# A two-layer graph kernel: earlier gathers, a product moved behind the last sums, and the feature halves formed inside the sweep

## The chip, the cores and the metric

One core of a Trainium2 chip runs the whole program. The metric is the device time of one execution in microseconds (us), as the median of three.

## The reference, cut to what matters

3125 nodes with 128 features, 103125 edges sorted by their target `dst`. Two layers follow each other:

```python
# layer 0
deg  = segment_sum(ones, src);  d = where(deg > 0, rsqrt(deg), 0)
h    = x @ weight
out0 = segment_sum((d[src] * d[dst])[:, None] * h[src], dst) + bias
x    = layernorm(x + out0)
# layer 1
w_ij  = mlp(edge_attr_64) + mlp(edge_attr_32)        # silu(x @ w0 + b0) @ w1 + b1
alpha = ((x @ wq)[dst] * w_ij * (x @ wk)[src]).sum(heads) / sqrt(16) * edge_weight
out1  = segment_sum(alpha * (x @ wv)[src], dst) / 16
x     = layernorm(x + out1)
```

## The kernel before, in words

The program has five stages. Engines run their own instruction streams and meet at semaphores; PE is the matrix engine, DVE the vector engine, ACT the scalar engine, POOL the GpSimd, SP a queue that only issues DMAs.

**Head (0 to 88 us).** The source degrees are counted with one-hot products (DVE line 1323, PE line 1033). DVE and ACT form `xs`, the features of all 25 blocks of 128 nodes times `dinv` (lines 1349 and 858), and ACT's queue stores them to `xs_d` in four DMAs (lines 862 and 865, semaphore `s_xs`). POOL prepares rows and the split of the MLP weights (lines 732 to 772). DVE decides how many passes a sweep needs (`passes_i`, one for these inputs, line 1376); every engine loads that number into a register before its loop. ACT rounds all of `xs` into `xs_hi` (line 873, 128x3200, fp32r) and loads the Silu table (line 874). DVE forms the rest `xs_lo = xs - xs_hi` in 13 instructions (line 1405), and then `start_pass1` (lines 1413 to 1428) writes rows, keys and bases of the pass; its last semaphore step `s_pass1` lets POOL start.

**Sweep 1 (88 to 568 us).** The sum of layer 0 over the edges, and a quarter of the MLP work of layer 1 on top, in 51 steps written out one behind the other. Of the 808 tiles of 128 edges, 358 are *gathered*: POOL issues one indirect DMA for each (line 794, seven a step, eight in the last), which fetches 128 rows of `xs_d` into one of four buffers `gath1`, and PE adds them with a one-hot product (`sum1`, line 1092), whose window DVE adds to `acc` (line 1468). The other 450 tiles are *counted*: DVE writes two one-hots for each (`hots`, lines 1475 and 1476), PE multiplies them into counts (`count_batch`, line 1114), DVE adds these into `count` (line 1492). In every eighth step and in the last, PE multiplies the counts with `xs_hi` and `xs_lo` (`sum_spans`, line 1122, 50 matmuls, "the product"), DVE adds the three windows (`add_spans`), and ACT sets the three parts of `count` back to zero in this and the next two steps (`clear_counts`, line 930). The MLP of a step: SP loads the edge features, ACT and DVE split them (`split_hi` line 892, `split_lo` line 1454), PE `layer1` (lines 1066, 1068), ACT Silu (line 900), PE `layer2` (line 1084), ACT copies out (line 919), puts the bias into the bank again (line 884), SP stores to `w_d` (line 529).

POOL's order is: wait for the pass rows, then for each step wait for the indices (`s_idx1`) and, from the fifth step on, for the sum four steps back (`s_sum1`), then issue. SP loads the indices of a step (line 536) behind the features of the step before it.

In the last step the order on PE is product, `layer2`, `sum1`, `layer2`. The next stage waits on PE for the sums, the spans and the last copy to `w_sb`.

**Middle (568 to 630 us).** DVE makes the rows of sweep 2 (lines 1564 to 1570 and 1433). PE multiplies `acc` with the weight (`convolve`, line 1163), DVE adds and takes statistics (line 1604), ACT normalizes, PE transposes and projects, SP stores `kv_d` and `q_d`.

**Sweep 2 (630 to 1668 us)** and the **end**: attention over 202 groups of 512 edges, then the second normalization. The change does not touch them.

## Time and profile before

| | |
|---|---|
| median of 3 runs | 1691.49 us (1691.41 to 1692.15) |
| the profiled execution's own time | 1685.36 us |
| its span, first to last instruction | 1683.5 us |
| PE busy | 1535.1 us (91%) |
| DVE busy | 1356.2 us (81%) |
| POOL busy | 1215.7 us (72%) |
| ACT busy | 955.0 us (57%) |
| mean granted clock of PE | 0.980 |

Busy shares are averages over stages with different limits, so the stretch in question is read by itself. The profiled execution lies 6.13 us below the median.

### The profile page before, as it was taken

The page shows a single profiled execution, that of the slowest core. Times are in us where ns is not written, and L with a number is a line of the kernel's source. Part 1 is how long each engine was busy: PE and PEld are TensorE (multiplying, and loading weights), DVE is VectorE, ACT ScalarE, POOL GpSimd, SP SyncE. Part 2 cuts the span into 40 slices and gives each one's busy share as a digit, 9 for nine tenths or more (in the row PEclk, how much of TensorE's full clock was granted, in tenths as well). Part 3 has the DMA queues.
Part 4 walks back from the last instruction along what each step waited for, and adds up shares of the span by engine and source line. Part 5 has one row for each costly group of instructions (what it writes and reads, how often), then busy time and mean ns, then how long its engine had stood idle before and what let it go on. Part 6 is the DMA issues. An engine that isn't in the chain of part 4 may idle for free.

```text
span 1683.5 us, 43509 instructions
## 1 busy us (share of the span) xinstructions
PE 1535.1 (91%) x12636; PEld 1426.1 (85%) x12636; DVE 1356.2 (81%) x3810; ACT 955.0 (57%) x1410; POOL 1215.7 (72%) x1201
## 2 busy tenths in 40 slices
PE   4379999999999759999999999999999999999995
PEld 3267988888898749998989898989898989898995
DVE  9988779797887457887888787888787878887886
ACT  3344646566565465665656565655555656565664
POOL 5677777777777247777777777777777777777772
PEclk9999999999999889999999999999999999999998
DMA  4133334343433286666666666666666666666673
GB/s 123 39 97 108 109 102 116 108 121 103 116 108 97 64 231 170 189 190 172 186 183 184 174 186 173 185 182 180 180 180 180 184 178 185 181 186 179 183 190 115
DMA packets 176755, 257.32 MB, mean 153 GB/s; under 512 B 80278, under 2 KB 91213, under 8 KB 176476
## 3 DMA queue, kind: packets, MB, share of 16 engines
q0 software_dynamic: 50240, 129.44, 29.1%
q1 hardware_dynamic: 123100, 124.61, 25.0%
q10 hardware_dynamic: 3264, 1.64, 0.3%
q8 instruction: 48, 0.79, 0.2%
q14 instruction: 103, 0.84, 0.2%
HBM read 232.76 MB, written 22.79 MB: 152 GB/s over the span
## 4 chain that ended last, share of the span: by engine, by line
PE 66%; POOL 13%; issue 8%; DVE 7%; DMA 3%; ACT 1%; DVEq 1%; SPq 1%; POOLq 0%; ACTq 0%
PE bank L1084 33%; POOL arena L794 13%; PE bank L1092 12%; PE bank L1066 9%; PE bank L1068 4%; PE bank L1122 3%; PE bank L1218 3%; DVE arena L1323 2%; DMA arena<-xs_d,idx 1%; DMA idx<-in_src_e 1%; PE bank L1114 1%; DVE xsplit L1454 1%; DVE late L1670 1%; ACT nodes L948 0%; DVE red L1687 0%
## 5 line engine op out<-in xcount | busy, mean ns | idle before, releaser
L784 POOL DMA_INDIRECT arena<-kv_d,idx x808 | 802.5, 993 | 273.2 <-issue 259.8
L1084 PEld LDWEIGHTS bank<-w,hid 128*128 128x128 f32 x6464 | 781.9, 192 | 27.2 <-issue 1.9
L1084 PE MATMUL bank<-w,hid 128*128 128x128 f32 x6464 | 790.9, 276 | 0.0
L900 ACT ACTIVATE hid<-bank,b 128x512 f32<-128x512 f32 x808 | 500.6, 683 | 273.1 <-PE bank L1068 260.2
L794 POOL DMA_INDIRECT arena<-xs_d,idx x358 | 354.6, 991 | 128.8 <-issue 124.5
L1066 PE MATMUL bank<-xsplit,w_hi 128*128 128x512 f32 x808 | 347.7, 441 | 26.3 <-DVE xsplit L1454 26.3
L1454 DVE TENSOR_TENSOR xsplit<-xraw,xsplit 64x256 fp32r<-64x256 f32 x808 | 288.0, 414 | 7.3 <-ACT xsplit L892 1.0
L1092 PE MATMUL bank<-onehot,late 128*128 128x126 f32 x1616 | 219.2, 285 | 33.6 <-DVE late L1708 31.7
L1092 PEld LDWEIGHTS bank<-onehot,late 128*128 128x128 f32 x1616 | 196.7, 195 | 36.9 <-DVE late L1708 33.6
L892 ACT ACTIVATE xsplit<-xraw 64x1024 fp32r<-64x1024 f32 x202 | 210.7, 1044 | 2.6 <-DMA xraw<-in_sph_t 1.7
L884 ACT ACTIVATE bank<-b_full 128x512 f32<-128x512 f32 x199 | 119.3, 599 | 160.4 <-DVE late L1708 158.8
L1066 PEld LDWEIGHTS bank<-xsplit,w_hi 128*128 128x128 f32 x808 | 157.5, 195 | 50.1 <-DVE xsplit L1454 24.5
L1661 DVE TENSOR_SCALAR late<-late,iota_part 126x512 bf16<-126x512 bf16 x202 | 71.0, 352 | 115.5 <-PE bank L1218 113.9
L1068 PE MATMUL bank<-xsplit,w_lo 128*128 128x512 f32 x404 | 163.8, 405 | 0.0
L1492 DVE TENSOR_TENSOR count<-count,bank 128x300 f32 x225 | 103.9, 462 | 59.9 <-PE bank L1114 46.4
L1670 DVE TENSOR_TENSOR late<-arena,bank 128x512 f32<-128x512 f32 x202 | 137.8, 682 | 7.0 <-PE bank L1218 5.4
L1682 DVE TENSOR_TENSOR late<-late,bank 128x512 f32<-128x512 f32 x151 | 103.0, 682 | 47.8 <-issue 32.7
L1476 DVE TENSOR_SCALAR key_hot<-iota_key,key 128x300 bf16<-128x300 bf16 x450 | 140.9, 315 | 0.0
L1687 DVE TENSOR_REDUCE red<-late 128x32 f32<-128x512 f32 x202 | 137.1, 679 | 0.1
L919 ACT ACTIVATE w_sb<-bank 128x512 f32<-128x512 f32 x51 | 30.5, 598 | 163.3 <-PE bank L1084 163.3
L1475 DVE TENSOR_SCALAR low_hot<-iota_key,low_f 128x128 bf16<-128x128 bf16 x450 | 117.7, 262 | 3.2 <-issue 3.1
L1092 PE MATMUL bank<-onehot,arena 128*128 128x126 f32 x716 | 93.2, 278 | 17.3 <-DMA arena<-xs_d,idx 17.1
(159 smaller groups left out, 1358.6 us busy)
## 6 DMA issues: line engine op xcount, KB each, us to landing
xraw<-in_rad_t SPq DMA_DIRECT2D x207, 128.0 KB
xraw<-in_sph_t SPq DMA_DIRECT2D x414, 64.0 KB
late<-relrow_d SPq DMA_DIRECT2D x103, 256.0 KB, 3.9
w_sb<-w_d SPq DMA_DIRECT2D x52, 256.0 KB
w_d<-w_sb SPq DMA_DIRECT2D x51, 256.0 KB
arena<-kv_d,idx POOLq DMA_INDIRECT x808
arena<-xs_d,idx POOLq DMA_INDIRECT x358
qwin<-q_d SPq DMA_DIRECT2D x101, 31.5 KB
```

Of the source, the lines that this page charges most:

```text
L784: pool.indirect_dma_start(gath[:, k, t * width:(t + 1) * width], None, table, bass.IndirectOffsetOnAxis(ap=idx[:, pair.slot(4), j * TILES ...
L794: pool.indirect_dma_start(gath1[s.slot(RING1)][:, t * D:(t + 1) * D], None, xs_d, bass.IndirectOffsetOnAxis(ap=idx[:, s.slot(4), t:t + 1], ...
L892: act.activation(xsplit[0:RAD, s.slot(2), :, :], xraw[:, k, :, :], ACT.Copy).then_inc(mlp.s_hi, 1)
L900: act.activation(hid[:, s.slot(2), c, :], hid_ps[s.sub(4, c, 4 * s.total).slot(len(hid_ps))][:, :], ACT.Silu, bias=b0[:, c:c + 1]).then_in ...
L1066: mm = pe.matmul(to, w0_hi[:, m, cols], xsplit[:, b, m, :], start=True, stop=(m == 1))
L1068: mm = pe.matmul(to, w0_lo[:, m, cols], xsplit[:, b, m, :], start=False, stop=True)
L1084: mm = pe.matmul(w_ps[:, t * D:(t + 1) * D], hid[:, b, c, t * P:(t + 1) * P], w1[:, c, :], start=False, stop=(c == 3), skip_group_check=True)
L1092: return pe.matmul(bank[7][:, 0:3 * WIN], rows, onehot[:, b, k:k + 3, :].rearrange("p t n -> p (t n)"), start=(k == 0), stop=(k == n - 1), ...
L1454: last = dve.tensor_tensor(xsplit[RAD:P, b, m, half], xraw[:, k, m, half], xsplit[0:RAD, b, m, half].bitcast(F32), ALU.subtract)
L1476: last = dve.tensor_scalar(key_hot[:, at_tile + t, :], iota_key[:, :], key[:, ds(col, 1)], None, ALU.is_equal)
L1670: dve.tensor_tensor(prod[:, j, :].rearrange("p (t f) -> p t f", t=TILES), kv(g)[:, :, 0, :], q_ps[j][:, :].rearrange("p (t f) -> p t f", t ...
L1687: dve.tensor_reduce(red[:, j, :, :].rearrange("p t h -> p (t h)"), prod[:, j, :].rearrange("p (h d) -> p h d", d=HD), AX.X, ALU.add).then_ ...
```

## The change

- POOL no longer waits for the pass rows before its first gather. The wait stands before the fourth step's gathers, whose buffer shares memory with what `start_pass1` writes. The wait for `s_xs`, the stored features, stays.
- `xs_hi` is rounded in two parts, blocks 0 to 14 by POOL (behind its weight split, before its register load) and blocks 15 to 24 by ACT (before the two casts of the halves). The half indices now live in `w_sb`, since `xs_hi` shares memory with where they were.
- `xs_lo` is formed by DVE inside the sweep, in 13 instructions over the steps 1, 2 and 3. PE waits for it before a product, no longer before the sweep.
- DVE splits the features of steps 0 and 1 before `start_pass1`. ACT loads the Silu table behind its first two splits. PE does all of `layer2` of step 0 before the counts and the sum.
- In the last step PE does `layer2`, `sum1`, `layer2` first and the product last. DVE adds the last window, makes the rows of sweep 2 (`rows_of_sweep2`) and then adds the spans. ACT clears the third part of `count` for the product of step 48 in step 49, not in step 50.

```diff
@@ late / w_sb
-        half_i, to = part_i(late, to, 2 * DENSE)
+        half_i, _ = part_i(w_sb[:, :, :].rearrange("p k f -> p (k f)"), 0, 2 * DENSE)
@@ POOL
+            pool.wait_ge(s_cast, CAST.rows)
+            pool.wait_ge(s_pre, PRE.xs + 1)
+            own = slice(0, XS_ACT[0])
+            pool.tensor_copy(xs_hi[:, own, :], xs_sb[:, own, :]).then_inc(s_round, 1)
             pool.wait_ge(s_pre, PRE.passes)
             n_pass1 = passes(pool, 1)
             pool.wait_ge(s_xs, 64)
...
                 if not s.before(RING1):
                     pool.wait_ge(s_sum1, (s - RING1).tick + 1)
+                if s.c == RING1 - 1:
+                    pool.wait_ge(s_pass1, s.p * PASS1 + PASS1)
                 pool.sem_inc(s_go, 1)
...
             with pool.Fori(0, n_pass1) as p:
-                pool.wait_ge(s_pass1, p * PASS1 + PASS1)
                 steps1(sweep1, p)
@@ ACT
+            act.wait_ge(s_xsa, NB - XS_ACT[0])
+            act.wait_ge(s_cast, CAST.rows)
+            own = slice(XS_ACT[0], NB)
+            act.activation(xs_hi[:, own, :], xs_sb[:, own, :], ACT.Copy).then_inc(s_round, 1)
             act.wait_ge(s_pre, PRE.half)
             act.activation(low_f[:, :], half_i[:, 0, :], ACT.Copy).then_inc(s_cast, 1)
             act.activation(hi8[:, :], half_i[:, 1, :], ACT.Copy, scale=float(NARROW)).then_inc(s_cast, 1)
-            act.wait_ge(s_pre, PRE.xs + 1)
-            act.wait_ge(s_xsa, NB - XS_ACT[0])
-            act.wait_ge(s_cast, CAST.all)
-            act.activation(xs_hi[:, :, :], xs_sb, ACT.Copy).then_inc(s_table, 1)
-            act.activation(table[:, :], b0[:, 0:1], ACT.Silu).then_inc(s_table, 1)
...
                     split_hi(s + 1, mlp)
+                    if mlp is mlp1:
+                        act.activation(table[:, :], b0[:, 0:1], ACT.Silu).then_inc(s_table, 1)
                     silu(s, mlp)
...
-                for j in reversed(range(SPANS)):
-                    k = product(s - j) if s.c >= j else None
-                    if k and (j < OPEN or not k.is_last()):
+                for c in range(s.c - SPANS, s.c + 1):
+                    k = product(Step(c, p=s.p, total=UNITS)) if c > 0 else None
+                    for j in range(OPEN if k and k.is_last() else SPANS if k else 0):
+                        if min(c + j, max(c, UNITS - 2)) != s.c:
+                            continue
@@ PE
-            pe.wait_ge(s_split, 1)
...
-            def sum_spans(added):
+            def sum_spans(added, p):
                 pe.wait_ge(s_add, added)
+                pe.wait_ge(s_split, p + 1)
...
                 if s.before(1):
                     layer1(s, mlp1)
+                    layer1(s + 1, mlp1)
+                    layer2(s, mlp1, w1_ps[0])
+                    count_batch(own[0])
+                    count_batch(own[1])
+                    sum1(s)
+                    for batch in own[2:]:
+                        count_batch(batch)
+                    return
                 if s.is_last():
+                    layer2(s, mlp1, w1_ps[0], range(2))
+                    sum1(s)
+                    layer2(s, mlp1, w1_ps[0], range(2, 4))
+                    pe.wait_ge(s_acc1, s.tick + 1)
+                    pe.wait_ge(s_zero, s.p * CLEARS + CLEARS - OPEN)
+                    sum_spans((s.p + 1) * COUNTED, s.p)
+                    return
...
@@ DVE
-            dve.wait_ge(s_xs, 64)
-            dve.wait_ge(s_table, 1)
-            for b in range(0, NB, 2):
-                own = slice(b, min(NB, b + 2))
-                last = dve.tensor_tensor(xs_lo[:, own, :], xs_sb[:, own, :], xs_hi[:, own, :].bitcast(F32), ALU.subtract)
-            last.then_inc(s_split, 1)
...
+            def low_xs(s):
...
+                for b in range(2 * (s.c - 1), NB, 6):
+                    own = slice(b, min(NB, b + 2))
+                    last = dve.scalar_tensor_tensor(out=xs_lo[:, own, :], in0=xs_hi[:, own, :].bitcast(F32), scalar=minus[:, 0:1],
+                                                    in1=xs_sb[:, own, :], op0=ALU.mult, op1=ALU.add)
...
+                if s.is_last():
...
+                    add_window(bases[0], WIN, sum1_ps, s_sum1, s.tick + 1, s_acc1, s.tick)
+                    rows_of_sweep2(s.p)
+                    dve.wait_ge(s_acc1, s.tick + 1)
+                    add_spans(product(s), span_bases)
+                    return
...
+                if 1 <= s.c <= 3:
+                    low_xs(s)
...
             with dve.Fori(0, n_pass1) as p:
+                head = Step(0, p=p, total=UNITS)
+                split_lo(head, mlp1)
+                split_lo(head + 1, mlp1)
                 start_pass1(p)
```

The instruction order shows three places. First ACT ahead of the sweep, before:

```order
L868 ACTIVATE low_f<-late 128x450
L869 ACTIVATE hi<-late 128x450
L873 ACTIVATE xs_hi<-arena 128x3200
L874 ACT_TABLE_LOAD
L874 ACTIVATE table<-b 128x1
L434 TENSOR_LOAD passes_i
L434 ISA x2
L879 ACTIVATE b_full<-bank 128x128
```

And with the change:

```order
L879 ACTIVATE xs_hi<-arena 128x1280
L881 ACTIVATE low_f<-w_sb 128x450
L882 ACTIVATE hi<-w_sb 128x450
L438 TENSOR_LOAD passes_i
L438 ISA x2
L887 ACTIVATE b_full<-bank 128x128
L944 UNCONDITIONAL_BRANCH
L944 ISA
L900 ACT_TABLE_LOAD
L900 ACTIVATE xsplit<-xraw 64x1024
```

The rounding is smaller and comes first; a table load now stands before the first `xsplit`, and the one for Silu follows the second `xsplit`.

Second, ACT from the last Silu of step 49 to the end of the sweep, before:

```order
L900 ACTIVATE hid<-bank,b 128x512
L930 ACTIVATE count<-count 128x2800
L918 REGISTER_ALU
L919 ACTIVATE w_sb<-bank 128x512
L884 ACTIVATE bank<-b_full 128x512
L930 ACTIVATE count<-count 128x2800
```

And with the change:

```order
L908 ACTIVATE hid<-bank,b 128x512
L942 ACTIVATE count<-count 128x2800 x2
L928 REGISTER_ALU
L929 ACTIVATE w_sb<-bank 128x512
L892 ACTIVATE bank<-b_full 128x512
```

Two clears now stand before the copy and the bias of step 49. In step 50 one clear is left, before the last copy to `w_sb`, as before.

Third, PE in the last step with the change (before, the 50 matmuls of the product stood ahead of the first of these rows):

```order
L1095 MATMUL bank<-w,hid 128x128 x4
L1103 MATMUL bank<-onehot,arena 128x126 x8
L1093 REGISTER_ALU
L1095 MATMUL bank<-w,hid 128x128 x4
L1093 REGISTER_ALU
L1095 MATMUL bank<-w,hid 128x128 x4
L1155 ISA
```

The product follows the last row.

## Rows read from the trace of the kernel before

**Rows 1.** POOL in order of time: start us, us, engine line op.

```profile
87.80 1.31 POOL L794 DMA_INDIRECT arena<-xs_d,idx  x1 [20.01 <-issue]
...
550.20 0.97 POOL L794 DMA_INDIRECT arena<-xs_d,idx  x1 [0.30 <-issue]
```

**Rows 2.** The gathers' line, 85 to 570 us: ns min/median/max, first and last start.

```profile
L794 POOL DMA_INDIRECT arena<-xs_d,idx x358: 951/955/1427, 87.8 to 550.2; - x179
```

**Rows 3.** PE in order of time, `sum1` of steps 9, 11 and 47.

```profile
177.61 1.73 PE L1092 MATMUL bank<-onehot,arena 128*128 128x126 f32 x14
...
193.16 1.73 PE L1092 MATMUL bank<-onehot,arena 128*128 128x126 f32 x14
...
524.72 0.93 PE L1092 MATMUL bank<-onehot,arena 128*128 128x126 f32 x6 [1.41 <-DMA arena<-xs_d,idx]
```

**Rows 4.** Waits, 85 to 560 us: PE's for the gathered rows.

```profile
PE bank L1092 <- DMA arena<-xs_d,idx: 17.1, 16, 1.8
```

**Rows 5.** DVE in order of time, head and start of the sweep.

```profile
68.13 2.23 DVE L1349 TENSOR_TENSOR arena<-nodes,dinv 128x896 f32<-128x896 f32 x2
...
74.21 0.13 DVE L1378 TENSOR_SCALAR passes_i<-small 1x1 int32<-1x1 f32 x1
...
78.05 4.31 DVE L1405 TENSOR_TENSOR rounded<-arena,xs_hi 128x256 fp32r<-128x256 f32 x13 [1.32 <-ACT xs_hi L873]
82.28 0.23 DVE L1413 TENSOR_SCALAR base_i<-base_f,off 1x51 int32<-1x51 f32 x1
...
86.12 0.63 DVE L1428 TENSOR_TENSOR key<-key,arena 128x450 f32<-128x450 f32 x1
```

**Rows 6.** The stores of `xs_d` from ACT's queue: issue and landing.

```profile
L865 ACTq DMA_DIRECT2D xs_d<-arena x2: 566/879/1192, 69.7 to 71.4; - x2
...
DMA to landing us min/median/max: 3.8/4.6/5.4
```

**Rows 7.** POOL's elementwise instructions up to 80 us, busy us and mean ns.

```profile
L768 POOL TENSOR_TENSOR w_lo<-w_raw,w_hi 128x512 fp32r<-128x512 f32 x1 | 32.5, 32477 | 12.0 <-ACT w_hi L849 12.0
...
L746 POOL TENSOR_SCALAR key<-tile_f 128x450 f32<-128x450 f32 x1 | 1.6, 1607 | 0.1
...
L705 POOL CAST iota_key<-arena 128x300 bf16<-128x300 f32 x1 | 0.4, 435 | 0.1
```

**Rows 8.** PE in order of time, end of sweep 1.

```profile
550.94 0.68 PE L1114 MATMUL bank<-key_hot,low_hot 128*128 128x300 bf16 x4
...
562.85 1.95 PE L1084 MATMUL bank<-w,hid 128*128 128x128 f32 x16
...
566.42 1.95 PE L1084 MATMUL bank<-w,hid 128*128 128x128 f32 x16
569.46 2.04 PE L1163 MATMUL bank<-w_l_sb,acc 128*128 128x128 f32 x16 [1.09 <-ACT w_sb L919]
573.70 1.87 PE L1163 MATMUL bank<-w_l_sb,acc 128*128 128x128 f32 x8 [2.19 <-DVE nodes L1604]
```

**Rows 9.** ACT in order of time, end of sweep 1.

```profile
547.10 2.55 ACT L930 ACTIVATE count<-count 128x2800 fp32r<-128x2800 f32 x1
551.23 0.60 ACT L919 ACTIVATE w_sb<-bank 128x512 f32<-128x512 f32 x1 [1.58 <-PE bank L1084]
563.05 2.54 ACT L930 ACTIVATE count<-count 128x2800 fp32r<-128x2800 f32 x1 [8.14 <-PE bank L1122]
568.49 0.60 ACT L919 ACTIVATE w_sb<-bank 128x512 f32<-128x512 f32 x1 [2.90 <-PE bank L1084]
```

**Rows 10.** DVE in order of time, end of sweep 1.

```profile
567.50 0.28 DVE L1565 TENSOR_SCALAR base_f<-base_f,small 128x101 f32<-128x101 f32 x1
...
572.08 0.60 DVE L1604 SCALAR_TENSOR_TENSOR nodes<-bank,dinv,nodes 128x128 f32<-128x128 f32 x2
```

**Rows 11.** PE and its granted clock (third number) just before the sweep's end.

```profile
552.00:560.00 8.00, 4.96 (x32) 1.00 0.10 38
```

**Rows 12.** The chain of waits, the sweep's end: PE's last product.

```profile
555.04 7.97 PE bank L1122 x50
```

More of the change, by code:

```diff
@@ L241, in build @@
         small = sb("small", [P, 16])
+        minus = sb("minus", [P, 1])
         dinv = sb("dinv", [P, NB])
@@ L344, in build @@
         s_split = sem("s_split")
+        s_round = sem("s_round")
+        s_minus = sem("s_minus")
+        s_early = sem("s_early")
         s_biased = sem("s_biased")
@@ L1099, in sum1 @@
                     pe.wait_ge(s_acc1, s.tick)
-                if product(s):
+                if product(s) and not s.is_last():
                     pe.wait_ge(s_wide, (product(s).tick + 1) * SPANS)
@@ L1129, in sweep1 @@
                     layer1(s, mlp1)
-                if s.is_last():
-                    pe.wait_ge(s_acc1, s.tick)
-                    pe.wait_ge(s_zero, s.p * CLEARS + CLEARS - OPEN)
-                    sum_spans((s.p + 1) * COUNTED)
-                else:
-                    layer1(s + 1, mlp1)
-                    count_batch(own[0])
-                    if product(s):
-                        pe.wait_ge(s_acc1, s.tick)
-                        sum_spans(own[0].tick)
-                    count_batch(own[1])
+                    layer1(s + 1, mlp1)
[6 more added lines that the diff above has]
+                    return
+                if s.is_last():
+                    layer2(s, mlp1, w1_ps[0], range(2))
[5 more added lines that the diff above has]
+                    return
+                layer1(s + 1, mlp1)
+                count_batch(own[0])
+                if product(s):
+                    pe.wait_ge(s_acc1, s.tick)
+                    sum_spans(own[0].tick, s.p)
+                count_batch(own[1])
                 layer2(s, mlp1, w1_ps[0], range(2))
@@ L1397, in _ @@
             pre(dve.tensor_tensor(near[:, :], dst_f[:, COLS1:COLS], tile_f[:, :], ALU.subtract))
+            dve.memset(minus[:, :], -1.0).then_inc(s_minus, 1)
             v = pre(dve.memset(off[:, :], 0.0))
[L1401 to L1406 removed]
             pre_wait(v)
@@ L1493, in add_counts @@
                                   ALU.add).then_inc(s_add, 1)
+            def low_xs(s):
+                if s.c == 1:
+                    dve.wait_ge(s_xs, 64)
+                    dve.wait_ge(s_round, 2)
+                    dve.wait_ge(s_minus, s.p + 1)
+                for b in range(2 * (s.c - 1), NB, 6):
+                    own = slice(b, min(NB, b + 2))
+                    last = dve.scalar_tensor_tensor(out=xs_lo[:, own, :], in0=xs_hi[:, own, :].bitcast(F32), scalar=minus[:, 0:1],
+                                                    in1=xs_sb[:, own, :], op0=ALU.mult, op1=ALU.add)
+                if s.c == 3:
+                    last.then_inc(s_split, 1)
+                    dve.wait_ge(s_split, s.p + 1)
+                    dve.memset(minus[:, :], 0.0).then_inc(s_minus, 1)
@@ new lines, in rows_of_sweep2 @@
+            def rows_of_sweep2(p):
+                dve.tensor_scalar(base_f[:, :], base_f[:, :], small[:, 3:4], None, ALU.mult).then_inc(s_early, 1)
+                dve.tensor_scalar(small[0:PAIRS, 4:5], relrow0[:, 0, 0:1], small[0:PAIRS, 3:4], None, ALU.mult).then_inc(s_early, 1)
+                dve.wait_ge(s_early, p * EARLY + 2)
+                dve.tensor_tensor(by_pair(rel0[:, :]), by_pair(dst_f[:, :]), pair_bcast(base_f[:, :]), ALU.subtract).then_inc(s_early, 1)
+                dve.tensor_scalar(relrow0[:, :, :], relrow0[:, :, :], small[0:PAIRS, 4:5], None, ALU.subtract).then_inc(s_early, 1)
+                dve.wait_ge(s_early, p * EARLY + 4)
+                dve.tensor_scalar(relrow[:, :, :], relrow0[:, :, :], float(PARTS), None, ALU.mult).then_inc(s_early, 1)
+                dve.wait_ge(s_early, p * EARLY + 5)
@@ L1495, in sweep1 @@
             def sweep1(s):
                 own = batches(s)
+                if s.is_last():
+                    bases = load(base1_i, s.n, 1, NP - 1)
+                    span_bases = load(span_i, (product(s) * SPANS).n, SPANS, NP - 1)
+                    dve.wait_ge(s_acc1, s.tick)
+                    add_window(bases[0], WIN, sum1_ps, s_sum1, s.tick + 1, s_acc1, s.tick)
[3 more added lines that the diff above has]
+                    return
@@ L1497, in sweep1 @@
                 if s.before(1):
                     one_hot(s, GATHERED, tiles1(s)).then_inc(s_hot1, 1)
-                    split_lo(s, mlp1)
-                    split_lo(s + 1, mlp1)
                     for j in range(HOTS):
@@ L1562, in _ @@
                 dve.wait_ge(s_zero, p * CLEARS + CLEARS)
-            v_off = pre(dve.memset(off[:, :], 0.0))
-            v = pre(dve.tensor_scalar(base_f[:, :], base_f[:, :], small[:, 3:4], None, ALU.mult))
-            v_rb = pre(dve.tensor_scalar(small[0:PAIRS, 4:5], relrow0[:, 0, 0:1], small[0:PAIRS, 3:4], None, ALU.mult))
-            pre_wait(v)
-            pre(dve.tensor_tensor(by_pair(rel0[:, :]), by_pair(dst_f[:, :]), pair_bcast(base_f[:, :]), ALU.subtract))
-            pre_wait(v_rb)
-            v = pre(dve.tensor_scalar(relrow0[:, :, :], relrow0[:, :, :], small[0:PAIRS, 4:5], None, ALU.subtract))
-            pre_wait(v)
-            next_rows()
+            dve.memset(off[:, :], 0.0).then_inc(s_rows, 1)
+            dve.wait_ge(s_rows, 1)
             def statistics(c, row, s_row, rows_done, s_bn, s_mv):
@@ L1815 @@
 PASS2 = 3
+EARLY = 5
 class PRE:
```

## The prediction

> **What bounds the kernel now.** Busy shares come first on the page, and they mislead: PE is busy 91% of the span, but the part that the change touches is sweep 1 with its head and tail. There I read POOL in order of time. It issues its first gather at 87.80 us after 20.01 us of idleness, and its last at 550.20 [rows 1]. These are 358 gathers [rows 2], so 357 intervals of (550.20 - 87.80) / 357 = 1.295 us, while a single gather takes 0.955 us at the median and 0.30 us lie between two [rows 1, 2]. So POOL issues without a break for 463 us: a step of seven gathers is 9.07 us, and eight steps are 72.5.
>
> PE then: `sum1` of step 9 begins at 177.61 and of step 11 at 193.16 [rows 3], that is 7.78 us a step where it waits for nothing, and a product takes 7.9 [rows 12]. Eight steps with one product cost PE 8 x 7.78 + 7.9 = 70.1 us, 2.4 less than POOL. It falls behind at each product and catches up: all in all it waits 17.1 us for gathered rows [rows 4], and the last such wait is in step 47 (1.41 us, [rows 3]). From there the tail runs on PE alone. So the bound of sweep 1 is when POOL starts, plus 358 gathers, plus the tail behind step 47. PE, DVE and ACT only have to keep up.
>
> **The start.** The first gather comes 87.80 - 86.75 = 1.05 us after the last instruction of `start_pass1` [rows 1, 5]. With the change that wait is gone and the next condition is `s_xs`. Its last store is issued at 71.4 and lands at most 5.4 us later [rows 6], at 76.8. `passes_i` is written at 74.34 [rows 5], so POOL has 2.5 us for its register load. With the same 1.05 us the first gather starts at 77.9: **9.9 us earlier**. The new wait before the fourth step asks for `start_pass1`, done near 86, and POOL gets there at 77.9 + 3 x 9.07 = 105, so it costs nothing.
>
> POOL first has to round 1920 columns. It can begin at 70.4, when DVE has written its part of `xs` (68.13 + 2.23, [rows 5]). The nearest row is a cast with one input, 300 columns in 0.435 us [rows 7], which makes 2.8 us in proportion and ends at 73.2, before 74.34: nothing. The far end is the scalar operation on 450 columns in 1.61 us [rows 7]: 6.9 us, ending at 77.3, which with a register load of 1 to 2 us costs 2 us, or up to 4.6 if DVE's small instructions meanwhile wait for it. I take zero, since the cast is the same kind of operation. The Trainium skill (GPSIMD Engine Reference, section 3.1, elementwise) has one-input bodies at 1.03 cycles an element, an estimate of 1.7 us; the result would be the same.
>
> **Gathers beside more DVE work.** The first gather takes 1.31 us beside `split_lo`, against 0.951 at the least [rows 1, 2], 0.36 extra. Now they run beside `start_pass1` too (4.5 us, from 82.28 to 86.75 [rows 5]), and in steps 1 to 3 beside 13 more instructions of 0.33 us (4.31 / 13, [rows 5]). At 0.2 us for about five gathers, I take **1.0 us** lost; bounds 0 and 3. The rule against the change is in the Trainium skill (SBUF — State Buffer, "SBUF: two separate sides"): while DVE runs in a two-port mode, GpSimd cannot write the descriptors of its DMAs at all. By that rule the first gathers would lose all the one-input time of `start_pass1`, an estimate of 2.6 us, and the sum would be 1.6 worse. The first gather's 0.36 us beside a run of DVE work says that it is less here.
>
> **PE and DVE at the start.** ACT gets a table load ahead of its first split, so the splits are ready near 79 and 80. DVE splits until 81.8, then `start_pass1` until 86.3, and starts its one-hots only 3 us earlier than before, while POOL is 9.9 ahead. PE's `layer1` starts near 80.4, `layer2` of step 0 fills until 90, and `sum1` of step 0 follows when its rows have landed (89). `xs_lo` adds 1.7 us of DVE work to step 1 and 1.3 to each of the two others. DVE is then at some 8.8 us a step against POOL's 9.07, so it neither gains nor loses; from step 4 on PE has 1.3 us of slack a step. POOL itself is held only if PE falls over 10 us behind. Cost: nothing, the cover is PE's 17.1 us of waiting [rows 4]; if that cover were gone, see the second rival. The 13 instructions leave the head, but the head's chain no longer ran over them for POOL: their 4.31 us are inside the 9.9, not added to them.
>
> **The tail.** In times of before: PE's counts end at 551.6 (550.94 + 0.68, [rows 8]). Both clears now stand ahead of the copy of step 49 on ACT: 547.10 + 2 x 2.55 = 552.2, then copy 0.60 and bias 0.60 [rows 9], so `layer2` of step 50 starts at 553.45. `layer2`, `sum1`, `layer2` take 1.79 each (562.85 to 566.42 is two of them, [rows 8]), until 558.85; the gathers have landed. The product ends 7.9 later, at 566.75. On ACT the clear of 2.54 us still stands between the product and the last copy, and this is late next: before, the copy waited for `layer2` and ended at 569.09 [rows 9]; now it ends at 566.85 + 2.54 + 0.6 = 570.05. `convolve` follows 0.37 behind it as before (569.46 - 569.09): 570.4, **1 us later** than before. But DVE was not ready before 572.08, since it made the rows of sweep 2 from 567.50 on (4.6 us, [rows 10]); these lie in the shadow of the product now. DVE's first row waits for half of the 2.04 us of `convolve` [rows 8]: 571.45. So 4.6 us of row work and 3.4 us of PE's idleness are taken away, and **0.6 us** comes out. If the granted clock falls during PE's new 3.6 us of idleness, eight of these matmuls cost 1.87 instead of 1.02 [rows 8], and 0.25 us is lost instead. Behind the idleness of 3.4 us before the product the granted clock was 1.00, that is 2.4 GHz [rows 11]; I take no fall.
>
> Sum: -9.9 + 1.0 - 0.6 = **-9.5 us**. The profiled execution's own 1685.36 becomes 1675.9, and the median, 6.13 above it, 1691.49 - 9.5 = 1682.0. Middle and sweep 2 move as a whole.
>
> **The rivals.**
> 1. *POOL's rounding is slow or held by DVE.* For it: line 768, also with an fp32r result, took 32.5 us [rows 7] beside DVE's one-hots. If the copy ends near 77.3 or only starts in DVE's gap behind 76.7, the gathers start 2 to 5 us later than 77.9, and the gain is 4.5 to 7.5: about 1685.5. The same page of the Trainium skill on the SBUF has the pair of ports held for a whole instruction by whoever comes first. Against: at 70.4 DVE has reductions with one input. Chance 0.12.
> 2. *PE or DVE becomes the bound of sweep 1.* If the lag from the start is never made up, only DVE's 3 us and PE's 7 count: gain 3 to 7, about 1686.5. Against: 17.1 us of waits. Chance 0.06.
> 3. *Slower: rounding to fp32r on POOL costs what line 768 shows by itself.* 32.48 us for 512 columns is 63 ns a column; 1920 columns are 122 us, from 70.4 to 192. The gathers would start at about 194 instead of 87.8, and the time would be about 1797. It decides from a copy of over 14 us, where the start falls behind 87.8. Against: line 768 ended about when DVE's one-hots did. Chance 0.03.
> 4. *The change doesn't do what it says*: PE stays 8 us behind at the end whatever POOL does, because the last product is too near. That is so before as well and moves along, so I give it 0.02, with 1690.
>
> **How the numbers follow.** Forecast 0.77, with its own range 1680 to 1684.5 from the bounds 0 and 3 of the contention and -0.6 to +0.25 of the tail. Down to 1679.5 and up to 1687.0 takes in rivals 1 and 2. A measurement of this kernel tells 0.2%, 3.4 us, from no change. Faster by more: 0.77 + 0.12 + 0.03 of rival 2 = 0.92. Within: 0.05. Slower: 0.03.
>
> **What would show it.** First gather near 78; POOL's cast under 4 us; last gather near 541; PE's last wait for gathered rows still near step 47; in the tail a product directly behind the last `layer2`, ACT's copy ending 3.3 us behind it, DVE's first row of the middle 0.6 us closer to the last gather (21.9 us before, 21.3 then). Wrong it is if the first gather comes later than 80, if gathers show idle times over 0.30 us in the sweep, or if PE waits for DVE at the first product.

## The result, and the profile after

| | before | after |
|---|---|---|
| median of 5 runs each | 1691.41 us (1690.00 to 1692.15) | 1678.05 us (1675.46 to 1682.64) |
| ratio | | 0.9926, 95% interval 0.9909 to 0.9943 |
| profiled execution | 1685.36 us | 1677.95 us |
| first gather, last gather | 87.80, 550.20 | 78.06, 541.60 |
| DVE's first row of the middle | 572.08 | 564.34 |
| first expansion of queries (PE, start of sweep 2) | 624.39 | 615.22 |

The change gains 13.4 us by these medians. I had forecast 9.5, and a range that ended at 1679.5: faster as forecast, and 1.5 us outside. Later comparisons ran the changed kernel 12 more times and the kernel before 92 more. Over all executions the means are 1679.7 (17) and 1691.1 (97), with a standard deviation of 3 us from one execution to the next on both sides: **11.4 us, give or take 1.5** (95%).

POOL in order of time in the changed kernel (start us, us, line and tiles, idle before), which answers to [rows 1, 7]:

```profile
70.66 1.78 POOL L783 CAST xs_hi<-arena 128x1920 fp32r<-128x1920 f32 x1 [2.74 <-DVE arena L1372]
78.06 1.20 POOL L804 DMA_INDIRECT arena<-xs_d,idx  x1 [5.61 <-issue]
79.56 1.19 POOL L804 DMA_INDIRECT arena<-xs_d,idx  x1 [0.30 <-issue]
...
541.60 0.96 POOL L804 DMA_INDIRECT arena<-xs_d,idx  x1 [0.30 <-issue]
```

The rounding takes 1.78 us and ends 1.9 us before `passes_i` is there. The first gather comes 9.74 us earlier, as worked out. The last comes 8.60 earlier. Its line, and the waits for gathered rows, answer to [rows 2, 4]:

```profile
L804 POOL DMA_INDIRECT arena<-xs_d,idx x358: 948/955/1439, 78.1 to 541.6; - x179
```

```profile
PE bank L1103 <- DMA arena<-xs_d,idx: 11.5, 11, 1.9
```

In the second line the numbers are us in total, times, and the longest. PE waits 11.5 us instead of 17.1, and still catches up behind each product. The tail on PE, with its granted clock, answers to [rows 8, 11]. First PE's order of time, then windows (us, PE busy, granted clock, DMA share, GB/s):

```profile
545.38 2.05 PE L1095 MATMUL bank<-w,hid 128*128 128x128 f32 x16 [1.71 <-ACT bank L892]
547.26 1.95 PE L1103 MATMUL bank<-onehot,arena 128*128 128x126 f32 x16
549.05 1.95 PE L1095 MATMUL bank<-w,hid 128*128 128x128 f32 x16
```

```profile
551.00:556.00 5.00, 5.00 (x35) 1.00 0.00 0
556.00:561.00 5.00, 2.70 (x18) 1.00 0.00 2
561.00:566.00 5.00, 3.56 (x17) 0.66 0.21 68
```

ACT and DVE beside it answer to [rows 9, 10]:

```profile
558.74 2.54 ACT L942 ACTIVATE count<-count 128x2800 fp32r<-128x2800 f32 x1 [13.49 <-PE bank L1134]
561.18 0.58 ACT L929 ACTIVATE w_sb<-bank 128x512 f32<-128x512 f32 x1
```

```profile
552.69 1.67 DVE L1536 TENSOR_SCALAR relrow<-relrow 101x1024 bf16<-101x1024 f32 x1
558.84 0.27 DVE L1486 TENSOR_TENSOR acc<-acc,bank 128x112 f32 x1 [4.48 <-PE bank L1134]
...
564.34 0.61 DVE L1653 SCALAR_TENSOR_TENSOR nodes<-bank,dinv,nodes 128x128 f32<-128x128 f32 x2 [2.76 <-PE bank L1186]
```

(The CAST is the rounding, L929 the copy to `w_sb`, L1653 DVE's first row of the middle.) The order is the forecast one: last sums, product at once behind them, the rows of sweep 2 (549.5 to 554.4) hidden. The product ends at 558.70, the clear and the copy follow it until 561.76, PE starts the middle at 562.14 after 3.44 us of idleness, and here the clock does fall (0.66 in the last window): the first 16 matmuls take 3.54 us where they took 2.04 [rows 8]. From the last gather to DVE's first row it is 22.74 us, not the 21.3 of the forecast.

So up to sweep 2 the two profiled executions differ by 9.2 us, and at the end by 7.4. The medians differ by 13.4. The experiments had to say which of these numbers the change owns.

### The profile page after: what moved, and what is told of

The parts are those of the page before. It is cut to its first block, busy times and chain, and to the rows that moved or that the text cites. A ratio compares the mean times of both kernels' runs of the same rounds, so it can differ in the third digit from the quotient of the medians.

```text
span 1676.1 us, 43517 instructions
## 1 busy us (share of the span) xinstructions
PE 1538.9 (92%) x12636; PEld 1429.3 (85%) x12636; DVE 1361.1 (81%) x3812; ACT 954.0 (57%) x1411; POOL 1217.6 (73%) x1202
## 4 chain that ended last, share of the span: by engine, by line
PE 69%; POOL 11%; issue 7%; DVE 4%; DMA 3%; ACT 2%; DVEq 1%; SPq 0%; POOLq 0%; ACTq 0%
PE bank L1095 35%; PE bank L1103 13%; POOL arena L804 11%; PE bank L1077 9%; PE bank L1079 4%; PE bank L1134 3%; PE bank L1241 3%; PE bank L1125 1%; DMA arena<-xs_d,idx 1%; DMA idx<-in_src_e 1%; DVE xsplit L1472 1%; DVE late L1719 1%; ACT nodes L960 0%; DVE red L1736 0%; DVE late L1757 0%
## 5 line engine op out<-in xcount | busy, mean ns | idle before, releaser
L1719 DVE TENSOR_TENSOR late<-arena,bank 128x512 f32<-128x512 f32 x202 | 137.7, 682 | 6.1 <-issue 4.5
L929 ACT ACTIVATE w_sb<-bank 128x512 f32<-128x512 f32 x51 | 30.5, 598 | 155.6 <-PE bank L1095 155.6
L1757 DVE TENSOR_TENSOR late<-arena,bank 128x512 f32<-128x512 f32 x151 | 102.5, 679 | 0.1
```

Source lines behind the costliest of these rows:

```text
L1719: dve.tensor_tensor(prod[:, j, :].rearrange("p (t f) -> p t f", t=TILES), kv(g)[:, :, 0, :], q_ps[j][:, :].rearrange("p (t f) -> p t f", t ...
```

## The experiments

Each run's median stands against the kernel before, timed on the same chip beside it:

| run | executions | median, us | ratio, 95% interval |
|---|---|---|---|
| before_again | 12 | 1690.26 | 0.9997 (0.9980 to 1.0015) |
| before_early | 12 | 1682.06 | 0.9953 (0.9937 to 0.9970) |
| after_hold | 12 | 1689.22 | 0.9988 (0.9973 to 1.0004) |
| tail_only | 12 | 1689.38 | 0.9988 (0.9975 to 1.0001) |
| early_tail | 6 | 1679.68 | 0.9936 (0.9917 to 0.9955) |
| after_oldtail | 12 | 1687.15 | 0.9970 (0.9952 to 0.9988) |
| after_again | 6 | 1678.05 | 0.9923 (0.9911 to 0.9935) |
| after_third | 6 | 1681.90 | 0.9946 (0.9926 to 0.9966) |
| before_fill | 12 | 1690.54 | 0.9999 (0.9983 to 1.0014) |
| copy_first | 6 | 1679.95 | 0.9938 (0.9913 to 0.9962) |
| before_long | 5 | 1682.74 | 0.9942 (0.9929 to 0.9955) |
| after_long | 4 | 1670.32 | 0.9868 (0.9852 to 0.9884) |
| copy_long | 5 | 1667.11 | 0.9856 (0.9843 to 0.9868) |
| copy_long2 | 5 | 1666.92 | 0.9866 (0.9839 to 0.9893) |
| early_copy_long | 5 | 1667.33 | 0.9870 (0.9844 to 0.9896) |
| late_idx | 5 | 1670.74 | 0.9880 (0.9855 to 0.9906) |

A difference of two means is given below with its 95% interval. The kernels ran on different chips, where the kernel before had means between 1690.2 and 1692.1 us, so 1 or 2 us between two runs of this table can be the chip's.

**Each kernel again.** No edit.

> The kernel before once more, unchanged, for a second profile and its spread. In the first profile the sweep over the 202 groups of the second half (sweep 2) took 1021 us, 45.4 us of it in ten disturbed steps at its loop turns, and that execution was 6.1 us faster than the median of the timed ones. Theory A (the change itself brings about 9 us, and the remaining 4 of the measured 13.4 lie in sweep 2, whose loop turns cost a varying 3 to 6 us each): median near 1691, and this profile shows the start of sweep 2 (first expansion of queries) at 624.4 within 0.3 us, whatever its total time; the total varies with sweep 2 alone. Theory B (head, sweep 1 or middle differ by as much from execution to execution): the first expansion moves by 1 us or more.

Median 1690.26 of 12 (1684.92 to 1695.08); first expansion at 623.86. Beside it and its three neighbours, 29 executions of the kernel before ran from 1683.11 to 1695.80. The 0.7 us between the three runs that the forecast was made on had been luck.

> The changed kernel once more, unchanged. The kernel before, run 29 times, has spread from 1683.1 to 1695.8 with a median of 1690.9. Theory A (the change brings about 9 us; the 13.4 of the first comparison was luck of five runs on each side, since each execution carries a varying sum from the ten loop turns of sweep 2): this median comes back between 1680.5 and 1683. Theory B (the change brings 13 us): 1678 again. In its profile first gather 78.1, last 541 within 1.5 us, convolution at half clock again or not according to the clock in the 3.4 us gap.

> The changed kernel a third time. So far 11 executions of it have a mean of 1678.8 (median 1678.05), the kernel before a mean of 1691.1 in 57, a difference of 12.4; yet the profiles have the first expansion of queries in sweep 2 only 9.1 us earlier (615.22 and 614.99 against 624.39 and 623.86). Theory A (the other 3 us are the chance of which sums of loop turns were drawn): mean of this run 1680 to 1683. Theory D (sweep 2 is really 3 us shorter in the changed kernel): 1678 to 1679 again.

The first repeat of the changed kernel gave 1678.05, the second 1681.90 (6 executions each), with first expansions at 614.99 and 612.89. One spoke for theory B, the other for A: neither 9 nor 13 us can be read from five or six executions.

**Where an execution's luck lies.** Sweep 2 turns its loop ten times. In the waits (engine, line, what it waited for: us, times, longest) of the kernel before (`before_again`) DVE's share of it is this line:

```profile
DVE late L1682 <- issue: 33.9, 10, 4.0
```

Around each turn DVE has 3 to 4 us without an instruction, PE then stands for 3 to 4 us, and the step of 19.5 us takes 3.0 to 6.7 us more. Two turns of that profile, by windows (us, PE busy, granted clock, DMA share, GB/s); the first lost some of its clock, the second none:

```profile
770.00:784.00 14.00, 10.10 (x69) 0.88 0.64 186
852.00:866.00 14.00, 10.34 (x84) 1.00 0.68 176
```

In the 12 profiles of kernels with this loop, 37 of 120 turns had no slow matmul on PE behind them and cost 3.27 us on average (2.99 to 3.86). The other 83, where split matmuls took 0.63 us instead of 0.40, cost 5.4 (4.4 to 6.7). The ten turns add up to 44.4 to 50.2 us in one execution. Which turns lose the clock differs from execution to execution, with the same kernel.

**The loop turns taken out.** The same edit in both kernels; the computation is the same.

```diff
-UNROLL2, LAST2 = 4, 4
+UNROLL2, LAST2 = 22, 4
```

> The kernel before with sweep 2's loop of 4 steps a turn made one of 22 steps a turn (two turns instead of eleven); the computation is the same. Theory A (each return of the loop costs DVE 3 to 4 us in which it has no instruction, and PE and the clock follow, 3 to 6 us each): 9 of the 10 disturbed steps become normal ones of 19.5 to 19.7 us, the spread from run to run falls from 12 us to under 4. The time falls by less than the 40 us so freed, because POOL issues its 808 gathers of sweep 2 without a pause, 5.19 us for a group of four against PE's 4.9: once its lead of 28 us is used up it sets the pace. I expect 4 to 12 us less than before: 1679 to 1687. Rival (the disturbance comes from something else that returns every fourth step, as the index or base loads): the ten disturbed steps stay, time unchanged.

> The changed kernel with the same loop of 22 steps a turn in sweep 2. With the loop turns gone, its difference to before_long shows what the change itself brings. Theory A: 8.5 to 9.5 us, 1670 to 1678. Theory B: 13.

In `before_long` the gap without an instruction on DVE is left once:

```profile
  issue: 3.9, 1
```

Of the 44 to 50 us of disturbance only 8.7 come out in the time (by means), as expected. The scatter did not fall as far as I expected: 3.6 us between the extremes of `before_long`, but 6.8 in the four executions of `after_long`. The wait that takes its place (ACT on the features' DMA, in `before_long` and then in `before_again`; in this view: busy us, mean ns, idle before and what ended it):

```profile
L892 ACT ACTIVATE xsplit<-xraw 64x1024 fp32r<-64x1024 f32 x147 | 154.5, 1051 | 77.8 <-DMA xraw<-in_sph_t 64.9 <-PE bank L1068 7.0 <-PE bank L1066 3.7
```

```profile
L892 ACT ACTIVATE xsplit<-xraw 64x1024 fp32r<-64x1024 f32 x147 | 153.5, 1044 | 2.9 <-DMA xraw<-in_sph_t 2.3
```

The two kernels are 12.4 us apart by medians, 11.8 by means (give or take 3.3, with so few runs), and their first expansions lie at 624.14 and 614.89, 9.3 apart.

**What holds sweep 2 then.** Edit, on the changed kernel with the long loop and ACT's copy moved (below):

```diff
-                    if j < len(ahead):
-                        load_idx(ahead[j], s_idx2, s_gath2, RING2)
                     load_rows(pair)
...
                         load_features(mlps[2], mlp2, first + 3)
+                    if j < len(ahead):
+                        load_idx(ahead[j], s_idx2, s_gath2, RING2)
```

> As copy_long2, and in sweep 2 SP loads the next step's gather indices behind the step's features instead of ahead of them. In copy_long SP waited 302 us, 78 times, at the index load for gathers to end, and ACT 74 us, 54 times, for features that were queued behind it, while the kernel before had 2 and 0.7 us there. Theory E (POOL's 808 gathers set the pace through SP's queue): the features come in time, PE runs 10 to 15 us further up to POOL's gathers, and the time falls by 5 to 12 us. Rival (POOL's pace binds at the next place, DVE's first product with the rows, at once; or POOL now waits for its indices): less than 2 us, or slower.

1670.74 against 1666.92 without the edit: slower by 3.8 us in the medians and by 2.9 (give or take 2.3) in the means, so its rival held. SP's own waits in `copy_long2`, without the edit, and then ACT's, and in `late_idx` the wait of DVE's first product with the rows:

```profile
SPq L525 <- DMA arena<-kv_d,idx: 304.9, 77, 5.6
```

```profile
ACT xsplit L900 <- DMA xraw<-in_sph_t: 80.5, 66, 2.9
```

```profile
DVE late L1722 <- DMA arena<-kv_d,idx: 58.2, 55, 3.6
```

With the queue in the one order the features wait behind gathers, with the other DVE waits for the gathers themselves. Either way POOL's 808 gathers, 5.17 to 5.19 us for a group of four, set the pace once the loop turns are gone: in the six profiles with the long loop the last of them starts 29.8 to 31.2 us ahead of the end, in the 12 with the short loop 30.2 to 39.3. So an earlier first gather goes through to the end.

**The early gathers alone**, on the kernel before:

```diff
                     pool.wait_ge(s_sum1, (s - RING1).tick + 1)
+                if s.c == RING1 - 1:
+                    pool.wait_ge(s_pass1, s.p * PASS1 + PASS1)
...
-                pool.wait_ge(s_pass1, p * PASS1 + PASS1)
                 steps1(sweep1, p)
```

> The kernel before with one part of the change: POOL's wait for the rows' bases stands before the fourth step, so the first three steps' gathers wait only for the rows. Everything else is as before (rounding on ACT, low halves and splits in DVE's head, the old tail). Theory A: first gather near 78, last gather near 541.6, 8.5 to 9.5 us earlier than before, provided that PE keeps up; PE's first gathered sum is held by DVE's head (one-hots ready near 90), so PE starts 10 us behind POOL and makes it up by step 20. Time 1691.4 - 9 = 1682 to 1683; with the extra 4 us of sweep 2, if these come with any earlier start, 1678. Rival (the moved head work is needed too: PE stays behind or POOL is held by the ring of four steps): last gather later than 545, time over 1685.

Mean 1681.5. First gather 77.93, last 539.44:

```profile
77.93 1.20 POOL L796 DMA_INDIRECT arena<-xs_d,idx  x1 [10.20 <-issue]
```

Most of the gain is in these three lines of code: 9.5 us (give or take 2.0) of 11.4 by means. In its one profile the first expansion comes at 613.59, where the four of the changed kernel have 612.89 to 615.22.

**The early gathers taken out**, all else of the change kept:

```diff
-                if s.c == RING1 - 1:
-                    pool.wait_ge(s_pass1, s.p * PASS1 + PASS1)
...
+                pool.wait_ge(s_pass1, p * PASS1 + PASS1)
                 steps1(sweep1, p)
```

> The changed kernel with POOL's wait for the rows' bases put back ahead of the first gather; all moved work stays where the change has it. Theory A: the first gather comes near 86.8 (bases ready near 85.5 plus 1.05, against 87.80 before), the last near 549, no gather slower than 1.0 us at the start, time 1.0 less than before through the start and 0.9 more through the tail: 1691, the gain gone. Theory C (the moved work by itself brings the 4 us that the early gathers do not explain): 1687.

Mean 1689.4; first gather 87.20, last 548.16; first expansion 621.18. That lies between the 1691 of theory A and the 1687 of theory C. Some 0.7 us of the 1.7 that are left of the gain (give or take 1.6) is the earlier first gather; the rest would be the tail's, but is too small for these times to show.

**The tail alone, and the tail with the early gathers.** `tail_only` is the kernel before with the change's hunks of `clear_counts`, PE's last step, DVE's last step and `rows_of_sweep2`; `early_tail` adds the early gathers.

> The kernel before with the new tail alone. My prediction had this part at -0.6, the profiles suggest +0.9: DVE's first row of the middle at 572.5 to 573 against 572.08 and 571.82, time 1691 to 1692. If the new tail shortens sweep 2 by 3 us: 1688.5.

> The kernel before with two of the three parts of the change: the early gathers, and the new tail (last product behind the last sums, clears reordered, rows of sweep 2 beside it). The work of the head stays where it was. Theory A: last gather near 541, DVE's first row of the middle near 564 as in the changed kernel (564.34 and 563.89), for the moved head work brings nothing; time within 1 us of the changed kernel in the same comparison. If sweep 2 is 3 us shorter because of the new tail: 1678.5; if it needs the moved head work: 1682.

`tail_only`: mean 1688.6, 2.5 us less than before (give or take 1.7); last gather to first row 22.57; first expansion 621.15. `early_tail`: mean 1679.5, 2.0 us less than `before_early` (give or take 2.3); 21.65, because here the clock held behind the product; first expansion 612.41. So the tail gains about 2 us, where the profiles had made me expect a loss of 1, though only the first of the two differences is clear of the noise. The number that I had tied to a shorter sweep 2 came (1688.5), but not for that reason: the gain stands ahead of sweep 2. The first expansion is 3.0 us earlier than in the profiles of the kernel before (mean 624.1), of which 0.9 is an earlier last gather, 0.8 the way from there to the first row, and 1.3 a shorter middle, each within what single profiles of one kernel differ by. With the two parts together the changed kernel's time is reached within 0.1 us (give or take 2.1): nothing shows that the moved head work is needed for it.

**The old tail in the changed kernel** (PE: product, then the last weights and sums; DVE: `rows_of_sweep2(0)` behind them).

> The changed kernel with the old tail: product, then last weights and sums, then the rows of sweep 2 on DVE behind them. Theory A: conv of the middle near 560.4, DVE's first row near 563, as in the run with the early gathers alone (563.00), that is 0.9 to 1.3 us earlier than with the new tail: the new tail costs 1 us. If the new tail shortens sweep 2 by 3 us: time 2 us above the changed kernel, 1680.5 to 1681; if not: 1 us below it, 1677.5.

Mean 1686.5: 6.8 us worse than the changed kernel (give or take 2.6; 5.1 beside `after_third` on the same chip), against my 1 us better. Its first expansion comes at 620.62, 6.1 us later than the changed kernel's mean. Of these, 1.6 are a late last gather (the gathers last 464.4 us, the longest of all), 3.6 lie between it and DVE's first row (26.2 us), and 1.0 in the middle. It isn't a clean undoing of the tail, as the rows of sweep 2 take longer than in the kernel before, one instruction above all; DVE in `after_oldtail`, then in `before`:

```profile
563.11 2.10 DVE L1531 TENSOR_TENSOR rel<-dst_f,base_f 128x808 f32<-128x808 f32 x1
```

```profile
567.81 1.00 DVE L1568 TENSOR_TENSOR rel<-dst_f,base_f 128x808 f32<-128x808 f32 x1
```

From the start of these rows to DVE's first row of the middle it is 6.0 us, against 4.6 before. Why that instruction takes 2.10 us is not shown, and with it this run can't price the old tail by itself.

**The old tail's clock.** I read the product of all profiles with the old tail. In the execution that the forecast was made on, its 50 matmuls take 7.97 us [rows 12]. In `before_again`, by the chain of waits, and in `before_early`, by windows:

```profile
553.47 9.29 PE bank L1122 x50
```

```profile
544.00:549.00 5.00, 4.55 (x19) 0.66 0.00 0
```

PE idles 3.42 to 3.56 us ahead of the product in all five, and in four of them (9.29, 9.50, 9.48 and 9.47 us) 9 to 12 matmuls in a row come every 0.28 us instead of 0.155: from the start or nearly so in `before_again` and `after_oldtail`, only from the seventh or eighth on in `before_early` and `before_long`. To try it, 20 matmuls that nobody reads fill the gap:

```diff
                     pe.wait_ge(s_acc1, s.tick)
+                    for h in range(20):
+                        pe.matmul(span_ps, xs_hi[:, h, :], xs_hi[:, 3:6, :].rearrange("p b f -> p (b f)")[:, 0:SPANS * WIDE],
+                                  start=True, stop=True, skip_group_check=True)
                     pe.wait_ge(s_zero, s.p * CLEARS + CLEARS - OPEN)
```

> The kernel before, where PE issues 20 extra matmuls, 128x336 like the product's, whose result nobody reads, in the 3.4 to 4.1 us in which it waits for ACT's clear ahead of the last product. Nothing else is changed. If the clock falls for that idleness: the granted clock stays 1.00 through the product, all its 50 matmuls take 0.155 us each (7.9 us in all, from start of the first to end of the last), and the last gather lies 21.9 to 22.6 us ahead of DVE's first row of the middle instead of 23.6 and 24.5; time 1 to 2 us less than before. If the long first matmuls come from something else (the counts just cleared, the weights' loads): they stay at 0.28 us and the time is unchanged or up.

```profile
551.02 3.33 PE L1133 MATMUL bank<-xs_hi 128*128 128x336 f32 x20
554.71 0.42 PE L1122 MATMUL bank<-count,xs_hi 128*128 128x336 f32 x1 [0.36 <-ACT count L930]
```

```profile
555.00:560.00 5.00, 5.00 (x34) 1.00 0.01 3
```

The clock stays at 2.4 GHz, the product takes 7.93 us, and the first row comes 22.70 us behind the last gather. One execution can't tell this from the one in five where the clock held without the filling. The first expansion lies at 623.15, 1.0 us earlier than in the other three. The times can't show a microsecond.

**The new tail's gap closed.** The same cause in the changed kernel: ACT's clear stands between the product and the copy on which PE's first matmul of the middle waits.

```diff
                 activate(s, mlp1)
-                clear_counts(s)
+                if not s.is_last():
+                    clear_counts(s)
...
+                if s.is_last():
+                    clear_counts(s)
```

> The changed kernel, where in the last step ACT copies the last weights out of PSUM ahead of its clear of 2.54 us, which stood before that copy. If the tail of the change is late because PE's first matmul of the middle waits for this copy (561.18 + 0.58) behind the clear: PE's convolution starts near 560.5 instead of 562.1, runs at 1.00 granted clock (2.0 us for 16 matmuls instead of 3.54) since PE idles 1.8 us instead of 3.4, and DVE's first row of the middle comes near 562 instead of 564.3: time 2.0 to 2.6 us less than the changed kernel, 1675.5 to 1676. If DVE's wait for the clear or the clock sets the row anyway: less than 0.7 us.

```profile
550.28 0.60 ACT L930 ACTIVATE w_sb<-bank 128x512 f32<-128x512 f32 x1 [5.87 <-PE bank L1098]
557.91 2.54 ACT L945 ACTIVATE count<-count 128x2800 fp32r<-128x2800 f32 x1 [7.03 <-PE bank L1137]
```

```profile
559.58 2.04 PE L1189 MATMUL bank<-w_l_sb,acc 128*128 128x128 f32 x16 [1.71 <-DVE acc L1489]
```

The first row comes 19.92 us behind the last gather instead of 22.6, the gap is 1.71 us and the clock stays. The time, 1679.95, did not show it. With the long loop I tried again:

> As after_long, with the last step's weights copied ahead of ACT's last clear. The profile of the changed kernel with this copy alone had DVE's first row of the middle at 560.87 (564.34 without) and its 16 first matmuls of the middle in 2.04 us (3.54 without), yet its median of 6 was 1679.95, no better than the changed kernel's 1678.05 of 5. Theory A (spread of sweep 2 hid it): 2.5 to 3.5 us less than after_long. Rival (the gain of the head of the middle is given back by a later wait, as the stores to the table of keys and values): less than 1 us less.

> The changed kernel with ACT's last copy ahead of its clear and sweep 2's loop of 22 steps a turn, once more, as the base of the next two. 1667.1 again within 1.5 us.

1667.11 and 1666.92 against 1670.32: 3.3 us by medians, where the profiles have 2.7 at the first row. By means it is 2.9, give or take 3.2, with four executions of `after_long`; the sign is the expected one in both runs, but the times alone don't show it. The profiles do up to the start of sweep 2: first expansions at 611.33 and 610.89 against 614.89. Beside `before_long` this kernel is 15 us faster, beside the kernel before with its short loop 1.3 to 1.4%.

**The moved head work**, left out of that kernel:

> As copy_long2, but with the head's work (rounding, low halves, splits, PE's first step) left where the kernel before has it: only the early gathers and the new tail of the change. If the moved head work is worth nothing beside the early gathers (12 executions of the kernel before with the early gathers alone lost 1.0 us of gather time against the 2.4 of the changed kernel): last gather near 540.0 against 540.7, time equal within 1 us, or 1 us less. If it is worth something: 1 to 3 us more than copy_long2.

1667.33 against 1666.92, 0.5 us by means (give or take 2.5). Gathers last 461.1 us against 462.0, and the last comes at 539.53 against 540.03. No gain from it is seen here; one of a microsecond would not be.

## Why the prediction was right or wrong

From here on the first number of a pair is from the profiles of `before`, `before_again` and `before_long`, the second from those of `after`, `after_again`, `after_third` and `after_long`, each a mean.

- **The start** (forecast -9.9): first gather 87.9 and 78.1, -9.8. POOL's rounding (zero taken; it takes 1.78 us and ends in time), `s_xs` as the next condition and the 1.05 us behind it all held. So did the step that the new wait costs nothing. The Trainium skill's figure (GPSIMD Engine Reference, section 3.1) had given an estimate of 1.7 us for the rounding; the trace agrees.
- **Gathers beside more DVE work** (forecast +1.0, bounds 0 and 3): 461.1 us from first to last, and 462.9: +1.7. Under-sized by 0.7, with 2 us between the profiles of one kernel. The early gathers alone lose less than I took: 461.5 in `before_early`, 461.8 and 461.1 in the two with the new tail as well. The other part comes with the moved work. The five gathers that start beside `split_lo` and `start_pass1` take 1.03 to 1.30 us each, where most take 0.95; that is 1.1 us in all. The Trainium skill's rule (SBUF — State Buffer, "SBUF: two separate sides"), by which they would have lost all of the one-input time there, estimated at 2.6 us, asks for more than these rows show; whether DVE's instructions there ran in a two-port mode, no row shows.
- **The tail** (forecast -0.6): from the last gather to DVE's first row 23.3 and 22.6, -0.7, but the two steps behind it were wrong and cancelled. "I take no fall" was one: the clock falls in the new 3.44 us gap in all four profiles (16 matmuls in 3.5 to 3.8 us instead of 2.04), which makes the first row about 0.9 later. The other was to read the old tail from one execution: its 7.97 us for the product was the exception, 9.3 to 9.5 us came in the other four, so the old tail is 1.3 to 1.5 us longer as a rule. That the two cancelled was luck. The old product also has ACT's clear ahead of it, and so is not tied to the last gather: in `before_again` that comes 2.05 us earlier than in `before`, and the product's end 0.26. In the changed kernel it is tied: the product ends 16.9 to 17.1 us behind the last gather in all four. By the times the tail is worth more than my 0.6: 2.5 us, give or take 1.7, in `tail_only`.
- **"Middle and sweep 2 move as a whole"**: the middle, from DVE's first row to the first expansion, takes 51.8 and 50.9 us, between 50.2 and 52.3 in single executions, which I read as chance. At the start of sweep 2 the change has 9.6 us (624.1 and 614.5). The forecast sum was 9.5, so up to here it held in size, in part by luck.
- **From there to the medians** is where the forecast ended 1.5 us outside. The failed step is "the median, 6.13 above it, 1691.49 - 9.5 = 1682.0" with a range made of the mechanism's bounds alone: it has no term for how one execution, and so a median of a few, differs from the next. Its own bounds give 1681.0 to 1684.8, not 1680 to 1684.5, and the low end of 1679.5 is laid to rivals that are all slower than the forecast. Sweep 2 draws ten turns of 3.0 to 6.7 us anew in each execution, single times have a standard deviation of 3 us, and the median of five one of more than 1. The three times before, within 0.7 us, hid that. The kernel before happened to measure its long-run mean (1691.4 and 1691.1), the changed one 1.6 us less than its own (1678.05 and 1679.7). That part of the miss is chance; 1679.7 would have been just inside.
- **What stays open**: 11.4 in the times against 9.6 at the start of sweep 2. The difference of 1.8 us has an uncertainty as large, and may be nothing. From the first expansion to the end it is 1059.1 and 1062.7 us in `before` and `before_again`, 1060.9, 1059.0 and 1066.0 in `after`, `after_again` and `after_third`, which shows no shorter sweep 2. But its gathers on POOL are done sooner. In `before`, then in `after` (ns min/median/max, first and last start):

```profile
L784 POOL DMA_INDIRECT arena<-kv_d,idx x808: 945/949/1427, 604.5 to 1652.1; - x162
```

```profile
L792 POOL DMA_INDIRECT arena<-kv_d,idx x808: 942/949/1460, 596.1 to 1641.9; - x162
```

  They take 1047.6 and 1047.3 us in the two profiles of before, and 1045.8, 1046.1 and 1045.9 in the three of the changed kernel (1047.7 in `before_early`, 1046.8 and 1046.7 in `tail_only` and `early_tail`): 1.6 us less, and the last gather is 10.7 us earlier. That has the size of what is missing. What makes them faster, and how much of it reaches the end, no experiment here separates.
- **The rivals** of the prediction: slow rounding, a bound on PE or DVE, a start at 194 us, a change without effect: none happened. PE waited for nothing at the first product (159.1), and 11.5 us of waiting for rows were left as cover, in the one profile of `after`.
- Of what I said would show it: cast under 4 us, first gather near 78, last near 541, seen. PE's last wait for rows in step 47: in `after` only 0.4 us there, the last of more than half a microsecond in step 39, at 443; in the three other profiles again in step 47, of 1.2, 1.3 and 0.7 us. ACT's copy 3.3 us behind the product: 3.06. Row 0.6 us closer to the last gather: not seen in the pair of profiles, 0.7 in the means.

## What to carry to other kernels

Where one engine issues without a break for hundreds of microseconds, look for what its first instruction really needs; three lines that moved one wait brought 9.5 of 11.4 us, the new tail about 2, and the head work moved along with them nothing that these runs can show. Read a short stretch behind an idle PE from several executions before pricing it, since the clock may or may not fall there, and close such gaps by letting the copy that PE waits for pass the clear that nobody waits for. Before giving a range for a time, ask how much one execution differs from the next, not how far the first three were apart.

## What the runs showed of the hardware

- PE's idleness of 3.42 to 3.56 us ahead of the old product was followed by half clock in 4 of 5 profiles, at the product's start or up to 1.1 us into it, and one of 3.43 to 3.47 us ahead of the middle in 6 of 7; behind 0.36, 1.09 and 1.71 us of it in none, behind 1.84 us in part (`early_copy_long`, 16 matmuls in 2.58 us). With the gap filled by unused matmuls the clock stayed, in one profile.
- A turn of the loop with a 4-step body costs DVE 3 to 4 us in which the profile shows no instruction there, and so does the one turn with a 22-step body (3.1 to 3.9 us in six profiles).
- A rounding copy on POOL, 1920 columns with one input, takes 1.78 us, while 512 columns with two inputs beside DVE's one-hots took 32.5 us [rows 7].
